# Where two heads' P transposes stand in a slot, and the type in which they are done

## The reference

```python
qkv = x @ w_qkv.T + b_qkv                         # x: (8, 512, 1024), layer-normalised
q, k, v = to_heads(q), to_heads(k), to_heads(v)   # 8 heads of 64
scores = jnp.einsum('bhfc,bhtc->bhft', k, q)
scores = jnp.where(causal[None, None], scores, MASKED_BIAS)
attn = jax.nn.softmax(scores, axis=-2)            # this is P
vals = jnp.einsum('bhft,bhfc->bhtc', attn, v)
```

## Time and profile before

| | |
|---|---|
| median of 3 runs | 1449.1 us |
| the profiled execution | 1449.89 us |
| its span, first to last instruction | 1447.8 us |
| granted TensorE clock, mean | 0.999 of full speed |
| PE busy | 1430.7 us, 99% of the span |
| DVE, ACT, POOL busy | 63%, 48%, 43% |
| the loop body, seven passes | about 101.4 us each |

### The profile page before, as it was taken

One profiled execution on the slowest core, in us unless ns is written; L12 is line 12 of the kernel. 1 busy time (PEld: TensorE's weight loads), 2 busy tenths in 40 slices (PEclk: granted clock), 3 DMA queues, 4 the chain that ended last, 5 costly groups with the idle time before them and its releaser, 6 DMA issues.

```text
span 1447.8 us, 24821 instructions
## 1 busy us (share of the span) xinstructions
PE 1430.7 (99%) x7852; PEld 1272.1 (88%) x7852; DVE 918.8 (63%) x2118; ACT 692.6 (48%) x1497; POOL 625.7 (43%) x1154
## 2 busy tenths in 40 slices
PE   7999999999999999999999999999999999999998
PEld 6888888888888888888888889999999999999998
DVE  7576675675775775765755886555555555555554
ACT  6375465564573664754654863333333323333332
POOL 3353452461553453534523674444444334444442
PEclk9999999999999999999999999999999999999999
DMA  7333323223233223333223622222222222222211
GB/s 247 124 95 84 118 71 120 87 82 117 91 91 106 94 76 112 94 85 115 71 77 91 212 87 100 103 103 102 101 93 82 92 101 95 93 101 101 94 70 61
DMA packets 63636, 146.25 MB, mean 101 GB/s; under 512 B 6896, under 2 KB 28912, under 8 KB 63600
## 3 DMA queue, kind: packets, MB, share of 16 engines
q1 hardware_dynamic: 63600, 145.80, 30.7%
HBM read 60.06 MB, written 25.69 MB: 59 GB/s over the span
## 4 chain that ended last, share of the span: by engine, by line
PE 97%; DVE 1%; DMA 1%; ACT 0%; POOL 0%; issue 0%; DVEq 0%; POOLq 0%; SPq 0%
PE ps_f L2018 26%; PE ps_o L1382 20%; PE ps_o L1413 12%; PE ps_o L1970 11%; PE ps_s L1433 6%; PE ps_v L1260 4%; PE ps_o L1376 3%; PE ps_v L1261 3%; PE ps_t L1291 2%; PE ps_f L1999 2%; PE ps_t L1293 2%; PE ps_o L1336 2%; PE ps_o L1452 1%; PE ps_x L1989 1%; PE ps_t L1382 1%; PE ps_t L1269 1%
## 5 line engine op out<-in xcount | busy, mean ns | idle before, releaser
L2018 PE MATMUL ps_f<-wagh,x2Th 128*128 128x364 f32 x768 | 254.8, 332 | 1.1 <-DVE wagl L779 1.1
L2018 PE MATMUL ps_f<-wagh,x2Tl 128*128 128x364 f32 x768 | 252.6, 329 | 0.0
L2018 PE MATMUL ps_f<-wagl,x2Th 128*128 128x364 f32 x768 | 252.2, 328 | 0.0
L1382 PE MATMUL ps_o<-xTh,wh 128*128 128x512 f32 x424 | 173.5, 409 | 0.0
L1382 PE MATMUL ps_o<-xTh,wl 128*128 128x512 f32 x424 | 166.5, 393 | 0.0
L1382 PE MATMUL ps_o<-xTl,wh 128*128 128x512 f32 x424 | 165.6, 391 | 0.0
L2018 PEld LDWEIGHTS ps_f<-wagh,x2Th 128*128 128x128 f32 x768 | 144.2, 188 | 2.6 <-DVE wagl L779 1.4
L2018 PEld LDWEIGHTS ps_f<-wagl,x2Th 128*128 128x128 f32 x768 | 144.5, 188 | 1.1
L2018 PEld LDWEIGHTS ps_f<-wagh,x2Tl 128*128 128x128 f32 x768 | 144.4, 188 | 0.0
L541 POOL TENSOR_TENSOR cw<-wm,cnt 128x4 f32<-128x4 f32 x64 | 12.9, 201 | 296.9 <-ACT pr L1044 296.9
L564 POOL TENSOR_SCALAR pr<-pr,rden 128x512 f32<-128x512 f32 (+3 forms) x256 | 135.5, 547 | 0.0
(11 more groups left out here) (224 smaller groups left out, 3474.6 us busy)
## 6 DMA issues: line engine op xcount, KB each, us to landing
p_words<-pr SPq DMA_DIRECT2D x42, 448.0 KB, 2.7
kst<-kst SPq DMA_DIRECT2D x64, 256.0 KB, 3.7
xt<-in_x SPq DMA_DIRECT2D x32, 512.0 KB, 4.1
x2r<-x2n SPq DMA_DIRECT2D x30, 512.0 KB, 2.9
xs<-in_x SPq DMA_DIRECT2D x24, 512.0 KB, 4.5
out<-x SPq DMA_DIRECT2D x23, 512.0 KB, 3.0
valsT<-vt SPq DMA_DIRECT2D x64, 128.0 KB, 2.3
vraw<-valsT SPq DMA_DIRECT2D x32, 256.0 KB, 3.5
```

The costliest lines, as they stand in the source:

```text
L1382: done = pe.matmul(ps[:, :], w[:, k, c:c + P], xT[:, k, :], start=(k == 0 and w is wh and xT is xTh), stop=(k == KD - 1 and w is wl), skip ...
L2018: last = pe.matmul(ps_f[:, g, 0:GW], a[:, k, :], w[:, k, cols], start=(k == 0 and a is xh and w is wagh), stop=False, skip_group_check=True)
```

## The change

- All eight heads' P are copied into `p_words` and transposed from there; the list `MOVED` goes, and the copies count on two semaphores, one for each half of `p_words`, instead of one.
- In slots 6 and 8 transpose groups 0 and 1 are issued behind the second piece of projections instead of ahead of it.
- Head 7's group 2 moves from the end of slot 8 into slot 9, between the first half of its projection and `masked_weights(7)`.
- ACT's and DVE's lists for head 7 follow: `p_hi(7, 0..1)` and `p_lo(7, 0..1)` come after the slot's value and key work, and the group 2 pieces open slot 9.

```diff
-    MOVED = (0, 1, 2, 3, 4, 6)
...
-        p_moved = sem("p_moved")
+        p_moved = [sem(f"p_moved{i}") for i in range(2)]
...
                     if 2 <= h < 6 or h > 7:
                         store_vals(h - 2, b)
+                    if h == 7:
+                        dup_k(0, b + 1)
+                        store_vals(h - 2, b)
-                    if h in MOVED:
+                    if h < NH:
                         move_p(h, b)
...
# DVE (ACT alike, with p_hi)
-                    if 1 <= h <= NH:
+                    if 1 <= h < NH:
                         for g in range(2):
                             p_lo(h - 1, g, b)
+                    if h == NH + 1:
+                        p_lo(NH - 1, 2, b)
...
+                    if h == NH:
+                        for g in range(2):
+                            p_lo(h - 1, g, b)
...
# PE
+                    if n == 0 and part == 0 and h == NH + 1:
+                        transpose_p(pe, NH - 1, 2, b, True)
                     if n == 0 and part == 0 and h >= 2:
                         masked_weights(pe, h - 2, b)
...
-                    if 1 <= h <= NH:
-                        transpose_p(pe, h - 1, 0, b, h - 1 in MOVED)
-                        transpose_p(pe, h - 1, 1, b, h - 1 in MOVED)
+                    if 1 <= h < NH and h != BARE:
+                        transpose_p(pe, h - 1, 0, b, True)
+                        transpose_p(pe, h - 1, 1, b, True)
                     turns(h, 1, b)
                     steps(h, 1, b)
+                    if h in (BARE, NH):
+                        transpose_p(pe, h - 1, 0, b, True)
+                        transpose_p(pe, h - 1, 1, b, True)
                     turns(h, 2, b)
                     if h + 1 in AHEAD:
                         scores(h + 1, b)
-                    if 1 <= h <= NH:
-                        transpose_p(pe, h - 1, 2, b, h - 1 in MOVED)
+                    if 1 <= h < NH:
+                        transpose_p(pe, h - 1, 2, b, True)
```

More of the change, by code:

```diff
@@ L402, in move_p @@
                 sp.wait_ge(p_begun, H + 1)
-                sp.dma_start(p_words[:, q, 0:S_OFF[0]].bitcast(F32), pr[:, q, 0:S_OFF[0]]).then_inc(p_moved, 16)
+                sp.dma_start(p_words[:, q, 0:S_OFF[0]].bitcast(F32), pr[:, q, 0:S_OFF[0]]).then_inc(p_moved[q], 16)
                 sp.wait_ge(p_ready, H + 1)
-                sp.dma_start(p_words[:, q, S_OFF[0]:].bitcast(F32), pr[:, q, S_OFF[0]:]).then_inc(p_moved, 16)
+                sp.dma_start(p_words[:, q, S_OFF[0]:].bitcast(F32), pr[:, q, S_OFF[0]:]).then_inc(p_moved[q], 16)
             def store_vals(h, b):
@@ L431, in body @@
                         load_x(3, b + 1)
-                    if h in (7, 9):
-                        dup_k((h - 7) // 2, b + 1)
-                    if 2 <= h < 6 or h > 6:
+                    if h == 9:
+                        dup_k(1, b + 1)
+                    if 2 <= h < 6 or h > 7:
                         store_vals(h - 2, b)
-                    if h in MOVED:
+                    if h == 7:
+                        dup_k(0, b + 1)
+                        store_vals(h - 2, b)
+                    if h < NH:
                         move_p(h, b)
@@ L862, in body @@
                         lows(h, 1, b)
-                    if 1 <= h <= NH and h not in (BARE, BARE + 1):
+                    if h == NH:
+                        for g in range(2):
+                            p_lo(h - 1, g, b)
+                    if 1 <= h < NH and h not in (BARE, BARE + 1):
                         p_lo(h - 1, 2, b)
@@ L1092, in body @@
                 for h in range(SLOTS):
+                    if h == NH + 1:
+                        p_hi(NH - 1, 2, b)
                     if h >= 2:
@@ L1127, in body @@
                         highs(h, 1, b)
-                    if 1 <= h <= NH and h not in (BARE, BARE + 1):
+                    if h == NH:
+                        for g in range(2):
+                            p_hi(h - 1, g, b)
+                    if 1 <= h < NH and h not in (BARE, BARE + 1):
                         p_hi(h - 1, 2, b)
@@ L1275, in transpose_p @@
                 if moved:
-                    pe.wait_ge(p_moved, 32 * (len(MOVED) * b + MOVED.index(h) + 1))
+                    pe.wait_ge(p_moved[h % 2], 32 * (4 * b + h // 2 + 1))
                 else:
```

## The result

The changed kernel takes 1455.59 us (median of 5 runs, 1455.35 to 1456.01) against 1449.43 us (median of 5, 1448.25 to 1449.55) for the kernel before: +6.2 us, a ratio of 1.0043 with a 95% interval from 1.0032 to 1.0054. It is slower, by 0.4%.

A forecast was written before the change was run, and what follows sets the result against it. PE was taken to bound the kernel (97% of the span). A loss of 0.84 us per pass over seven passes, +5.9 us, gave 1455.8, or 1455.0 us against the median; 8 in 10 range 1451.2 to 1458.0.

The forecast's parts named there:

- The wait in slot 8: PE waits for q_lo(0) from DVE before the query projection, which starts only 0.06 us earlier than before.
- The idle time: PE idles up to 1.2 us per pass ahead of slot 8's projection, part possibly ahead of head 6's values.
- Slot 6: Key projection goes first, the waits for P and the copy vanish; PE is 0.45 us early after group 2.
- The type's share: Transposing from p_words instead of fp32 saves 0.36 us of PE work per pass, 2.5 us over the loop.
- Slot 8 and 9: Transposes behind the projection take 0.66 us, then a wait ahead of masked_weights(7); the pass loses 0.84 us.
- The 0.08 us on the ACT and DVE chain: Delay of the chain from head 5's last p_hi to q_lo(0), bounds 0 and 0.18 us.
- PE's busy time: Sign in the changed profile: PE's busy time falls by about 2.5 us while the span grows by about 6.
- The faster one: Rival: the chain to q_lo(0) comes earlier with PE, gaining 0.3 to 0.56 us per pass, 1445.2 to 1447.0; 7%.
- The no-change one: Rival: shorter idle ahead of slot 8's projection, no wait at masked_weights(7); +0.1 to +0.3 us per pass, 1449.8 to 1451.2; 12%.
- the new wait: In slot 9 PE waits 0.26 us per pass ahead of masked_weights(7), until DVE has emptied ps_t[1].
- The late copy of head 5: Rival: the copy lands after 3.1 us, delaying slot 6's transposes; 1.2 to 1.4 us lost per pass, 1457.7 to 1459; 10%.

The follow-up runs named there:

- e3: The changed kernel with q_hi(0) moved to the start of ACT's slot 7 and q_lo(0) ahead of reciprocal(7) on DVE, PE untouched; 1451.57 us.
- e2: The changed kernel with head 5 put back ahead of its projection, fp32 and not copied, so only head 7's part remains; 1455.51 us.
- e1: The kernel before with only head 5's part: its transposes behind the key projection and from the copied P; 1449.87 us.
- e4: The changed kernel with its new places kept, but heads 5 and 7 transposed as fp32 straight from pr, without copies; 1457.50 us.
- e6: e5 with head 7's eight transposes issued behind nine of the projection's twelve matmuls in slot 8; 1449.24 us.
- e9: e5 with masked_weights(7) issued three matmuls later in slot 9, transposes left in place; 1447.20 us.
- e5: The changed kernel with q_hi(0), vals_lo(5) and vals_sum(5) moved earlier on ACT and DVE, and q_lo(0) behind head 6's last p_lo; 1447.45 us.
- e8: The kernel before with e5's shortened ACT and DVE chain alone, no transposes moved or retyped; 1448.71 us.

## Why the prediction was right

*The wait in slot 8.* Right, with its place, its releaser and its own time: `q_lo(0)` was put 0.08 us later on its chain and came 0.07 us later (232.50 against 232.18, less the offset of 0.25; counted from the pass's start it is 0.02 us, so shifts this small depend on where one starts to count), and PE followed its end by 0.06 us as forecast. e3 shows that this wait is what most of the loss hangs on, e2 that it needs only head 7's half of the change.

*The idle time.* I had put up to 1.2 us on it, possibly in two parts, and as a sign of it 0.8 to 1.2 us of idle time ahead of the projection. That sign didn't come as put: the lists have 0.49 us there on PE and 0.75 us on its weight loads. It came in two: head 6's values start 231.83 - 229.87 = 1.96 us after `masked_weights`, where the kernel before needed 1.57 us for the like stretch, 0.39 us of it lost; and the projection 0.71 us after the last value matmul instead of 0.06, 0.65 us lost: 1.04 us together. That the first of the two takes all that slot 6 gives, so that the second doesn't depend on head 5 at all, I had not worked out; e1 and e2 show it.

*Slot 6.* Right in kind: no wait for P, no wait for the copy, transposes at 218.21 (217.92 forecast, and 0.25 of offset). The projection took 2.84 us and not 2.80, and group 2 waited a little for DVE (the weight loads' list has 1.1 us over seven passes, where the kernel before has none), so the gain was 0.37 us and not 0.45. The size of that gain doesn't matter for the total, as e2 shows. The type's share was read a little high: the 0.85 us of eight fp32 transposes in slot 6 stand behind a wait, and 0.06 of it belongs to that; without one they take 0.79 us, in e4 too.

*Slot 8 and 9.* The transposes 0.64 us (236.93 to the next start at 237.57), 0.66 forecast. `masked_weights(7)` starts at 239.41, where 239.15 would have been its turn: 0.26 us of wait, as forecast. From there to head 7's values 1.63 us instead of 1.57. That makes 0.89 us where the prediction had 0.84; over the seven passes 0.90 us each, +6.3, of which the medians show 6.2. I forecast +5.9. The 0.08 us on the ACT and DVE chain was picked between 0 and 0.18; that it fits to 0.01 us is luck. What it is made of did come as told: head 5's first `p_hi` starts at 218.70, where 218.43 and the offset give 218.68.

*What failed.* The time held, but beside the idle time just told one more sign did not. I said that PE's busy time would fall by about 2.5 us. It rose, from 1430.7 to 1431.6 us. The page of the changed kernel:

```profile
PE 1431.6 (99%) x7852; PEld 1269.8 (87%) x7852; DVE 918.1 (63%) x2118; ACT 693.5 (48%) x1497; POOL 625.7 (43%) x1154
```

The step that failed is the reading of busy time as work. PE's records overlap, and only their union is counted: a matmul of 0.39 us costs 0.23 where the next one follows, but all of its 0.39 count when PE then waits. The three waits of a pass thus add uncovered ends to the busy time, about 0.16 us each or an estimated 3.4 us over seven passes (1.04 us lost at two of them show up as only 0.49 + 0.22 us of idle, 0.26 at the third as 0.09: it ends at 239.03 + 0.29 and PE goes on at 239.41). With the places kept (e4, busy 1434.5 us) the type does take 2.9 us off the busy time.

*The rivals.* The faster one needed the chain to move with PE. Its condition stands there twice, as 0.45 us and as about 1 us; by the prediction's own figures it is 1.10 us, since PE comes to the projection at 232.65 and so `q_lo(0)` has to end by 232.59 instead of 233.69. The chain didn't move: exponentials of head 7 start at 227.46, 0.10 us later than before (less the offset), behind DVE, whatever PE had gained. The no-change one fell with the 0.64 us of transposes and the new wait, which came in full. The late copy of head 5 did not occur; e6 shows what a late copy looks like, on head 7.

*What stays open.* Why e1's pass is longer than the mechanism gives (by 0.1 us by the trace, by 0.03 us by the medians), and whether e9 is faster than e5, are both below what these runs can tell. What head 7's half gives alone under the short chain was not run.

## What to carry to other kernels

On an engine that is never idle, work that stands ahead of a wait may be filling it: before moving it, look up what the next instruction waits for and when that ended. Here 0.79 us of transposes covered a wait whose releaser ended 0.20 us before their end, so moving them cost all of their time, and the gain made elsewhere in the pass went into the same chain. The remedy was to shorten the chain of the other two engines with idle time that they had, and only then did the moved and cheaper transposes pay, by about 0.1% (e5's median is 1.8 us below that of the kernel before beside it and 1.3 us below e8's).

## What the runs showed of the hardware

- In groups of eight, transposes of 128x128 fp32 blocks start 0.109 us apart, those in the rounded type 0.085 us (medians over the kernel before): a ratio of 1.3. Up to the start of what follows, such groups differ less, 0.79 against 0.64 to 0.67 us, a ratio of 1.2, since the next instruction starts 0.03 us behind the last fp32 transpose and 0.09 us behind the last of the other type.
- PE's first matmul after an idle time is slower to be followed. At 231.83 in the changed kernel the next starts 0.31 us later (232.14), in steady flow 0.23 us, and it is 0.30 or 0.31 us in all seven passes. Behind the other two waits it is 0.28 us instead of 0.17 for `masked_weights`, and 0.33 us instead of 0.29 (e3, where the projection follows the values without a wait) for the projection. So each of these waits costs 0.04 to 0.11 us more than its length, which PE's idle figure doesn't show.
- The 192 KB copies in SBUF landed 2.4 us after their issue in the median. In e6 head 7's transposes start 2.58 us after POOL is through with head 7's P (230.78 + 2.06 = 232.84, and 235.42); PE came to them 2.08 us after it and waited, in every one of the seven passes.
